# Logits blocks that contract 64 partitions each, from alternating halves, in a graph kernel on one core

## The chip, the cores and the metric

One Trainium2 chip (trn2), one core of it. The metric is the device time of one execution in microseconds (us). Before the change three executions took 1065.97, 1066.78 and 1067.74 us, median 1066.78 us.

## What is computed

Four graph layers run one after the other on 2048 nodes with 128 features, each behind a layer normalisation, a ReLU and a residual sum. The change lies in the second one, an attention with nucleus (top-p) sparsification, done twice:

```
for n in range(2):
    q = Xa @ W1.T @ W2.T                  # 2048 x 64
    k = Xa @ W3.T                         # 2048 x 64
    probs = softmax(q @ k.T)              # 2048 x 2048 logits, contracted over 64
    A = probs kept up to a mass of 0.9 per row, renormalised
    Xf = R @ Xf;  Xa = A @ Xa
    Z = Z + Xf @ U1[n].T + Xa @ U2[n].T
```

R is the row-normalised adjacency matrix plus identity. Everything is float32.

## The kernel before, in words

Each engine has its own program, written out by hand in order; semaphores tie them together. A program's order is thus the queue of its engine. The 2048 nodes are 16 tiles of 128 rows; four tiles are a group, numbered gi from 0 to 7 over the two steps of the attention.

**Keys.** The tile K (128 partitions, 2048 columns) holds the layer's input until it has been saved to memory, and then the keys. `keys_of` and, for step 1, `later_keys` (L652, L881) multiply W3 with 512 nodes and give 64 rows; ScalarE copies them (`keys_of`, L1141) to the partitions 0 to 63 of K and adds them up on the way into `ksum4`, of which `ksum` is the sum. GpSimd writes zeros to the partitions 64 to 127 of K, once (`keys_zeroed`, L453), each block after its saving DMA, and to the same partitions of ST[1] (L467). It does so between the `power` instructions that the layer normalisations wait for. TensorE waits for these zeros by `zero_ok` (L890, L899).

**Queries.** `queries` (L692) multiplies W1 with the group's 512 nodes (64 rows out), ScalarE copies them to ST[0], TensorE multiplies with W2 (L710, contracted over 64 partitions, 64 rows out), ScalarE copies the result to the partitions 0 to 63 of ST[1]. `means` (L713) multiplies the queries with `ksum` for the mean logit of each row, a column at a time; VectorE scales it by 1/2048 (L1679).

**Logits.** One tile of 128 rows has 2048 logits in each row: four matmuls of 512 columns into four neighbouring PSUM banks, L743 in `logits`, L728 in `logit_part` for the first two tiles of a step. With the zeros below, each contracts all 128 partitions. A float32 matmul stands in the trace as two weight loads (LDWEIGHTS) and two MATMUL instructions in turn, so that a tile's logits are 8 MATMULs. VectorE then takes the row maximum over the four banks (L1659, `row_max`), ScalarE the exponential (L1217). But for the first groups of a step, where tiles alternate between banks 0 to 3 and 4 to 7, all tiles use banks 0 to 3, so the logits of one tile wait until the exponential of the tile before it has left the banks.

**What runs beside them.** While the logits of group gi+1 are made, VectorE finds the thresholds of group gi by sums over 2048 elements (L1520, some of them on ScalarE, L1249) and sorted maxima (L2106), and TensorE does `attend` for the group before: for each tile it turns the kept probabilities in 4x4 transposes (L546), ScalarE copies each (L1082), and 16 matmuls follow (L808). The logits of the tiles 1 to 3 of a group stand inside `attend`, ahead of its `mults(0)` (L821); those of tile 0 stand behind the group's queries and means. In the first group of each step there is no `attend`, and units of the product R @ Xf (L612) stand between the logits.

The prologue that leads to the first logits is the first layer's product (L676), with the keys of blocks 0 and 1 and the first query (L655, L660) put between its matmuls by `MEANWHILE`. It waits for six copies of turned weights by ScalarE (`wt_ok`, L639, L1113 to L1118).

Of the kernel before, what the change touches and what calls it, by code (L numbers as in the profile page):

```python
# [14 lines left out]
P = 128  # L15
# [79 lines left out]
def gnn_kernel(nc, x, adj, W0, b0, W1, W2, W3, U1, U2, ln_g, ln_b, L2W, L3W, b3, out):  # L95
# [18 lines left out]
    with ExitStack() as ctx:  # L114
# [15 lines left out]
        XR = XT[:, :].rearrange("p (t c) -> p t c", c=P)  # L130
        keys = K[0:DA, :, :].rearrange("p t c -> p (t c)")
        wide_keys = K[:, :, :].rearrange("p t c -> p (t c)")
        ST = [sb(f"ST{i}", [P, BK]) for i in range(2)]
# [88 lines left out]
        def rows(b):  # L222
# [11 lines left out]
            sure_steps ksum_ok mean_mm mean_ok lnz_ok gap_ok guess_steps guess_ok  # L234
            cs_ok at_saved un_half un_st un_t un_row un_pr un_z th_ok sum_ok roots_ok fin_sq bias_ok h2_t h2_st hw_mm x2_ok mask_ok zero_ok
            ln_steps ln_sq ln_var ln_pow ln_root ln_y ln_t ln_ts ln_x ln_x2 h2_act diag_ok early_in x2_dma"""
# [7 lines left out]
         ksum_ok, mean_mm, mean_ok, lnz_ok, gap_ok, guess_steps, guess_ok,  # L244
         cs_ok, at_saved, un_half, un_st, un_t, un_row, un_pr, un_z, th_ok, sum_ok, roots_ok, fin_sq, bias_ok, h2_t, h2_st, hw_mm, x2_ok, mask_ok, zero_ok,
         ln_steps, ln_sq, ln_var, ln_pow, ln_root, ln_y, ln_t, ln_ts, ln_x, ln_x2, h2_act, diag_ok, early_in, x2_dma) = [sem(n) for n in names.split()]
# [185 lines left out]
        def _(pool):  # L432
# [19 lines left out]
            n += 2  # L452
            def keys_zeroed(b, count):  # L453

                pool.wait_ge(x1_dma[b], 16)
                if count > 0:
                    pool.wait_ge(zero_ok, count)
                pool.memset(K[DA:P, b * G:(b + 1) * G, :], 0.0).then_inc(zero_ok, 1)

            for b in range(NB - 1):  # L460
                power(sm[:, 3, :], sm[:, 2, :], 0, G, n + 1 + b)
            pool.wait_ge(pw_out, n + NB - 1)
            for b in range(NB - 1):
                keys_zeroed(b, b)
            pool.wait_ge(ps_t, 1 + NB)
            pool.wait_ge(zero_ok, NB - 1)
            pool.memset(ST[1][DA:P, :], 0.0).then_inc(zero_ok, 1)  # L467
            pool.wait_ge(zero_ok, NB)
            power(sm[:, 3, :], sm[:, 2, :], 0, G, n + NB)
            n += NB  # L470
            pool.wait_ge(pw_out, n)
            keys_zeroed(NB - 1, NB)
            pool.wait_ge(zero_ok, NB + 1)
            power(esc[:, :], cs[:, :], 1, NT, n + 1)
# [67 lines left out]
        def _(pe):  # L542
# [95 lines left out]

            pe.wait_ge(wt_ok, 6)  # L639

# [11 lines left out]
            def keys_of(n):  # L652

                pe.wait_ge(h_st, 1 + NB + n + 1)
                pe.matmul(bank(n)[0:DA, :], WT[:, W3T, 0:DA], XT[:, n * BK:(n + 1) * BK],  # L655
                          start=True, stop=True).then_inc(k_mm, 1)
# [5 lines left out]
            def second_query():  # L662

                pe.wait_ge(t1_out, 1)
                pe.matmul(bank(7)[0:DA, :], WT[0:DA, W2T, 0:DA], ST[0][0:DA, :], start=True, stop=True)\
                  .then_inc(q_mm, 1)
# [25 lines left out]
            def queries(step, g):  # L692
                src = XT if step == 0 else xaT
                gi = NB * step + g

                if gi - 1 in BOTH:
                    pe.wait_ge(exp_ok, G * gi)
                if gi > 0:
                    pe.wait_ge(q_out, gi)
                if gi > 2:  # L700
                    pe.wait_ge(z_ok, G * (gi - 1 if gi == NB + 1 else gi - 2))
                issued = units_by(NB * step + (1 if g == 3 else 0))
                if g == 2:
# [6 lines left out]
                pe.matmul(bank(7)[0:DA, :], WT[0:DA, W2T, 0:DA], ST[0][0:DA, :], start=True, stop=True)\  # L710
                  .then_inc(q_mm, 1)

            def means(step, g):  # L713


                gi = NB * step + g
                pe.wait_ge(q_out, gi + 1)
                pe.wait_ge(ksum_ok, step + 1)
                if gi > 0:
                    pe.wait_ge(mean_ok, gi)  # L720
                for k in range(G):
                    mm = pe.matmul(bank(6)[:, MEANS + G * (gi % 2) + k:MEANS + G * (gi % 2) + k + 1],
                                   ST[1][0:DA, k * P:(k + 1) * P], ksum[0:DA, :], start=True, stop=True)
                mm.then_inc(mean_mm, 1)

            def logit_part(k, n):

                return pe.matmul(bank(4 * k + n), ST[1][:, k * P:(k + 1) * P], wide_keys[:, n * BK:(n + 1) * BK],  # L728
                                 start=True, stop=True)

            def logits(step, g, k):
# [10 lines left out]
                for n in range(4):  # L742
                    mm = pe.matmul(bank(half(gi, k) + n), ST[1][:, k * P:(k + 1) * P],  # L743
                                   wide_keys[:, n * BK:(n + 1) * BK],
                                   start=True, stop=True)
                mm.then_inc(logits_ok, 1)
# [134 lines left out]
            def later_keys(n):  # L881

                pe.wait_ge(exT_ok, G * (n + 1))
                pe.matmul(bank(n)[0:DA, :], WT[:, W3T, 0:DA], xaT[:, n * BK:(n + 1) * BK],
                          start=True, stop=True).then_inc(k_mm, 1)

            for step in range(STEPS):
                if step == 0:
                    pe.wait_ge(q_out, 1)
                    pe.wait_ge(zero_ok, NB)  # L890
                    for n in range(3):
                        pe.wait_ge(k_out, n + 1)
                        logit_part(0, n)
                        if n < 2:
                            logit_part(1, n)
                    hr_turned(3)
                    keys_of(3)
                    pe.wait_ge(k_out, 4)
                    pe.wait_ge(zero_ok, NB + 1)  # L899
                    logit_part(0, 3).then_inc(logits_ok, 1)  # L900
                    means(0, 0)
                    logit_part(1, 3)
                    pe.wait_ge(mean_ok, 1)
                    logit_part(1, 2).then_inc(logits_ok, 1)
                    for k in range(2, G):
                        logits(0, 0, k)
                else:
                    later_keys(3)
                    pe.wait_ge(k_out, NB + 4)
                    logit_part(0, 3).then_inc(logits_ok, 1)  # L910
                    means(1, 0)
                    for n in (0, 1, 3):
                        logit_part(1, n)
                    pe.wait_ge(mean_ok, NB + 1)
                    logit_part(1, 2).then_inc(logits_ok, 1)
                    for k in range(2, G):
# [31 lines left out]
                if step == 0:  # L948
                    later_keys(2)
                    pe.wait_ge(q_out, NB + 1)  # L950
                    for n in range(3):
                        pe.wait_ge(k_out, NB + n + 1)
                        logit_part(0, n)
                    for k in range(G):
# [120 lines left out]
        def _(act):  # L1075
# [37 lines left out]
            copy(WT[:, 0, 0:DA], bank(4)[:, 0:DA]).then_inc(wt_ok, 1)  # L1113
            copy(WT[:, 1, 0:DA], bank(4)[:, P:P + DA]).then_inc(wt_ok, 1)
            copy(WT[0:DA, 2, 0:DA], bank(4)[0:DA, 2 * P:2 * P + DA]).then_inc(wt_ok, 1)
            copy(WT[:, 3, :], bank(4)[:, 3 * P:4 * P]).then_inc(wt_ok, 1)
# [24 lines left out]
            def keys_of(step, n):  # L1141

                act.wait_ge(k_mm, 4 * step + n + 1)
                act.activation(keys[:, n * BK:(n + 1) * BK], bank(n)[0:DA, :], ACT.Copy,
                               accum_out=ksum4[0:DA, n:n + 1]).then_inc(k_out, 1)

# [14 lines left out]
            act.wait_ge(q_mm, 1)  # L1161
            copy(ST[1][0:DA, :], bank(7)[0:DA, :]).then_inc(q_out, 1)
            for n in range(2, NB):
# [6 lines left out]
            def queries(step, g):  # L1170
# [4 lines left out]
                act.wait_ge(q_mm, gi + 1)  # L1175
                copy(ST[1][0:DA, :], bank(7)[0:DA, :]).then_inc(q_out, 1)

# [330 lines left out]
        def _(dve):  # L1508
# [73 lines left out]
            v(tt(XR, XR, BC[:, B0, :].unsqueeze(1).to_broadcast([P, NT, P]), ALU.add))  # L1582
            dve.wait_ge(wt_ok, 6)
            v(tt(WT[:, L2WT, :], WT[:, L2WT, :], ident[:, :], ALU.add))
# [878 lines left out]
```

## Time and profile before

| | |
|---|---|
| median of three executions | 1066.78 us (1065.97 to 1067.74) |
| span of the profiled execution, first to last instruction | 1063.4 us |
| TensorE busy, of the span | 838.8 us (79%) |
| VectorE busy | 779.5 us (73%) |
| ScalarE busy | 510.0 us (48%) |
| GpSimd busy | 69.7 us (7%) |
| mean granted clock of TensorE, of full speed | 0.899 |

The span is the only time of the profiled execution itself; the median of the timed ones is 3.4 us above it. Times in the rows below are microseconds from the span's start. In the trace's lists a row of an engine gives start, length, engine, line, operation, output and inputs with their shape, how many instructions are merged in it, and in brackets how long the engine had been idle and what released it. PEld is TensorE's weight load. A shape such as 64*128 ahead of the sizes is the part of the array that a matmul uses: contracted partitions times columns. The chain of waits is the sequence of work that ended last, followed back from the end.

### The profile page before, as it was taken

The page shows a single profiled execution, that of the slowest core. Times are in us where ns is not written, and L with a number is a line of the kernel's source. Part 1 is how long each engine was busy: PE and PEld are TensorE (multiplying, and loading weights), DVE is VectorE, ACT ScalarE, POOL GpSimd, SP SyncE. Part 2 cuts the span into 40 slices and gives each one's busy share as a digit, 9 for nine tenths or more (in the row PEclk, how much of TensorE's full clock was granted, in tenths as well). Part 3 has the DMA queues.
Part 4 walks back from the last instruction along what each step waited for, and adds up shares of the span by engine and source line. Part 5 has one row for each costly group of instructions (what it writes and reads, how often), then busy time and mean ns, then how long its engine had stood idle before and what let it go on. Part 6 is the DMA issues. An engine that isn't in the chain of part 4 may idle for free.

```text
span 1063.4 us, 12286 instructions
## 1 busy us (share of the span) xinstructions
PE 838.8 (79%) x3886; PEld 566.1 (53%) x3886; DVE 779.5 (73%) x2363; ACT 510.0 (48%) x979; POOL 69.7 (7%) x68
## 2 busy tenths in 40 slices
PE   5889958887887853939779878868658999996695
PEld 4844425655665642737256557547447475553342
DVE  5968779888987998971697899889789702326715
ACT  4877235357368376413552664674775232023212
POOL 0020110000000000000000000010001100002201
PEclk9899998998988995969799789989789999998798
DMA  9849304424004000000043320230260456500001
GB/s 339 344 174 431 119 8 151 132 106 159 1 1 159 1 0 2 1 2 1 1 158 124 108 88 1 79 136 1 59 269 15 153 238 253 221 1 0 1 0 40
DMA packets 20221, 108.25 MB, mean 102 GB/s; under 512 B 1824, under 2 KB 8752, under 8 KB 9776
## 3 DMA queue, kind: packets, MB, share of 16 engines
q1 hardware_dynamic: 18752, 106.77, 27.0%
q10 hardware_dynamic: 1392, 0.61, 0.2%
q8 instruction: 29, 0.48, 0.2%
q14 instruction: 48, 0.39, 0.1%
HBM read 88.23 MB, written 19.14 MB: 101 GB/s over the span
## 4 chain that ended last, share of the span: by engine, by line
PE 46%; DVE 27%; ACT 13%; issue 9%; POOL 2%; DMA 1%; DVEq 1%; POOLq 0%; SPq 0%; ACTq 0%
PE PS L808 10%; DVE AT L1520 8%; PE PS L743 6%; PE PS L676 5%; PE PS L546 5%; DVE mxv L1659 4%; PE PS L877 3%; ACT BC L1249 3%; ACT AT L1249 3%; DVE nd L1523 3%; PE PS L1060 3%; PE PS L1036 3%; PE PS L1066 2%; DVE AT L2106 2%; ACT AT L1082 2%
## 5 line engine op out<-in xcount | busy, mean ns | idle before, releaser
L1082 ACT ACTIVATE AT<-PS 128x512 f32<-128x512 f32 (+2 forms) x240 | 118.8, 561 | 121.3 <-PE PS L546 103.7
L743 PE MATMUL PS<-K,ST 128*128 128x512 f32 x224 | 125.6, 713 | 13.0 <-ACT EA L1217 7.6
L546 PE MATMUL PS<-ident,AT 128*128 128x128 f32 x544 | 85.5, 293 | 55.4 <-DVE rS L2161 24.5
L1520 DVE SCALAR_TENSOR_TENSOR AT<-EA,se 128x2048 uint8<-128x2048 f32 (+1 forms) x46 | 107.6, 2345 | 1.6 <-DVE se L1513 0.3
L546 PEld LDWEIGHTS PS<-ident,AT 128*128 128x128 f32 x544 | 68.7, 152 | 64.0 <-DVE rS L2161 26.1
L1520 DVE SCALAR_TENSOR_TENSOR AT<-AT 128x2048 uint8<-128x2048 f32 (+2 forms) x48 | 96.1, 2002 | 2.0 <-PE PS L546 1.1
L1659 DVE TENSOR_REDUCE mxv<-PS 128x1 f32<-128x2048 f32 x32 | 73.3, 2289 | 26.0 <-PE PS L743 20.4
L743 PEld LDWEIGHTS PS<-K,ST 128*128 128x128 f32 x224 | 49.4, 232 | 73.1 <-issue 73.0
L2106 DVE MAX8 AT<-AT 128x8 f32<-128x256 f32 x256 | 87.6, 412 | 0.7
L808 PE MATMUL PS<-hr,AT 128*128 128x128 f32 x512 | 69.8, 285 | 9.2 <-ACT AT L1082 8.4
L808 PE MATMUL PS<-AT 128*128 128x128 f32 x512 | 68.3, 281 | 8.7 <-ACT AT L1082 8.1
L808 PEld LDWEIGHTS PS<-hr,AT 128*128 128x128 f32 x512 | 64.6, 197 | 14.8 <-ACT AT L1082 12.0
L1082 ACT ACTIVATE ST<-PS 128x512 f32<-128x512 f32 (+3 forms) x43 | 23.9, 560 | 100.0 <-PE PS L1066 23.2
L808 PEld LDWEIGHTS PS<-AT 128*128 128x128 f32 x512 | 63.1, 194 | 14.8 <-ACT AT L1082 11.8
L612 PE MATMUL PS<-AT,hr 128*128 128x256 f32 x256 | 58.2, 380 | 1.6 <-ACT AT L1192 0.9
L612 PE MATMUL PS<-AT 128*128 128x256 f32 x256 | 58.0, 380 | 1.4 <-DMA AT<-keep_at 1.4
L676 PE MATMUL PS<-AT,R 128*128 128x512 f32 x128 | 56.8, 595 | 1.2 <-ACT WT L1082 1.2
L1036 PE MATMUL PS<-AT,R 128*128 128x512 f32 x128 | 57.2, 592 | 0.0
L1217 ACT ACTIVATE AT<-PS,negmax 128x2048 f32<-128x2048 f32 x16 | 31.5, 1966 | 48.8 <-DVE negmax L1517 48.8
L877 PE MATMUL PS<-AT,hr 128*128 128x512 f32 x96 | 46.0, 631 | 10.6 <-ACT hr L1355 10.6
L612 PEld LDWEIGHTS PS<-AT,hr 128*128 128x128 f32 x256 | 47.7, 190 | 11.3 <-issue 3.2
L612 PEld LDWEIGHTS PS<-AT 128*128 128x128 f32 x256 | 47.9, 190 | 10.5 <-issue 4.5
(297 smaller groups left out, 1473.1 us busy)
## 6 DMA issues: line engine op xcount, KB each, us to landing
AT<-keep_at SPq DMA_DIRECT2D x32, 1024.0 KB, 5.1
EA<-in_adj SPq DMA_DIRECT2D x20, 1024.0 KB, 6.8
keep_at<-AT SPq DMA_DIRECT2D x8, 2048.0 KB, 24.9
AT<-keep_at SPq DMA_DIRECT2D x8, 2048.0 KB, 12.3
AT<-in_adj SPq DMA_DIRECT2D x12, 1024.0 KB, 5.0
EA<-keep_degrees SPq DMA_DIRECT2D x1, 1024.0 KB, 6.5
keep_x<-K SPq DMA_DIRECT2D x4, 256.0 KB, 8.6
out<-EA SPq DMA_DIRECT2D x4, 256.0 KB, 2.3
```

Of the source, the lines that this page charges most:

```text
L546: return pe.transpose(dst, src, ident[0:p, 0:p])
L612: mm = pe.matmul(bank(6)[:, 2 * P:4 * P], left[:, j, :], slab[:, j, :], start=(j == 0), stop=(j == NT - 1))
L676: mm = pe.matmul(halves(4 + b % 2), R[:, j, :], AT[:, 2 * b:2 * b + 2, j, :], start=(j == 0), stop=(j == NT - 1))
L743: mm = pe.matmul(bank(half(gi, k) + n), ST[1][:, k * P:(k + 1) * P], wide_keys[:, n * BK:(n + 1) * BK], start=True, stop=True)
L808: mm = pe.matmul(bank(6)[:, 0:P], stg[b % 2][:, n * P:(n + 1) * P], left[:, j, :], start=(j == 0), stop=(j == NT - 1))
L877: mm = pe.matmul(bank(n), hr[:, t, :], natural(t)[:, n * BK:(n + 1) * BK], start=(t == 0), stop=(t == NT - 1))
L1036: mm = pe.matmul(halves(4 + i % 2), R[:, j, :], AT[:, 2 * b:2 * b + 2, j, :], start=(j == 0), stop=(j == NT - 1))
L1082: return act.activation(dst, src, ACT.Copy)
L1249: act.activation(act_junk[f], E[:, k, :], func, scale=-1.0, bias=th[:, k:k + 1], accum_out=below[:, f, k:k + 1]).then_inc(sum_ok, 1)
L1520: return dve.scalar_tensor_tensor(out=o, in0=x0, scalar=s, in1=x1, op0=op0, op1=op1, **k)
L1659: v(dve.tensor_reduce(mxv[:, odd:odd + 1], PS[:, b:b + 4, :], AX.XY, ALU.max))
L2106: v.put(dve.max(tops[0][:, k, s * TOP:(s + 1) * TOP], cands[k][:, s * N // SETS:(s + 1) * N // SETS]))
```

## The change

Keys and queries are made twice over: the copies of W3 and W2 stand twice in WT, so that the matmuls give 128 rows, and ScalarE copies 128 partitions. The logits matmuls of even blocks of 512 columns then contract the partitions 0 to 63, those of odd blocks 64 to 127. The means contract all 128 partitions, twice the sum, and are scaled by 0.5/2048. GpSimd's five memsets and the semaphore `zero_ok` go. ScalarE has two copies more at the weights, and `wt_ok` is waited for at 8.

```diff
-        keys = K[0:DA, :, :].rearrange("p t c -> p (t c)")
-        wide_keys = K[:, :, :].rearrange("p t c -> p (t c)")
+        keys = K[:, :, :].rearrange("p t c -> p (t c)")
...
-            for b in range(NB - 1):
+            for b in range(NB):
                 power(sm[:, 3, :], sm[:, 2, :], 0, G, n + 1 + b)
-            pool.wait_ge(pw_out, n + NB - 1)
-            for b in range(NB - 1):
-                keys_zeroed(b, b)
-            pool.wait_ge(ps_t, 1 + NB)
-            pool.wait_ge(zero_ok, NB - 1)
-            pool.memset(ST[1][DA:P, :], 0.0).then_inc(zero_ok, 1)
-            pool.wait_ge(zero_ok, NB)
-            power(sm[:, 3, :], sm[:, 2, :], 0, G, n + NB)
             n += NB
-            pool.wait_ge(pw_out, n)
-            keys_zeroed(NB - 1, NB)
-            pool.wait_ge(zero_ok, NB + 1)
...
-            pe.wait_ge(wt_ok, 6)
+            pe.wait_ge(wt_ok, 8)
...
-                pe.matmul(bank(n)[0:DA, :], WT[:, W3T, 0:DA], XT[:, n * BK:(n + 1) * BK],
+                pe.matmul(bank(n), WT[:, W3T, :], XT[:, n * BK:(n + 1) * BK],
...
-                pe.matmul(bank(7)[0:DA, :], WT[0:DA, W2T, 0:DA], ST[0][0:DA, :], start=True, stop=True)\
+                pe.matmul(bank(7), WT[0:DA, W2T, :], ST[0][0:DA, :], start=True, stop=True)\
...
-                                   ST[1][0:DA, k * P:(k + 1) * P], ksum[0:DA, :], start=True, stop=True)
+                                   ST[1][:, k * P:(k + 1) * P], ksum[:, :], start=True, stop=True)
...
-            def logit_part(k, n):
+            def logit_part(to, k, n):
 
-                return pe.matmul(bank(4 * k + n), ST[1][:, k * P:(k + 1) * P], wide_keys[:, n * BK:(n + 1) * BK],
-                                 start=True, stop=True)
+                half_rows = slice(0, DA) if n % 2 == 0 else slice(DA, P)
+                return pe.matmul(bank(to + n), ST[1][half_rows, k * P:(k + 1) * P],
+                                 keys[half_rows, n * BK:(n + 1) * BK], start=True, stop=True)
...
                 for n in range(4):
-                    mm = pe.matmul(bank(half(gi, k) + n), ST[1][:, k * P:(k + 1) * P],
-                                   wide_keys[:, n * BK:(n + 1) * BK],
-                                   start=True, stop=True)
+                    mm = logit_part(half(gi, k), k, n)
...
-                    pe.wait_ge(zero_ok, NB)
...
-                    pe.wait_ge(zero_ok, NB + 1)
...
-            copy(WT[:, 1, 0:DA], bank(4)[:, P:P + DA]).then_inc(wt_ok, 1)
-            copy(WT[0:DA, 2, 0:DA], bank(4)[0:DA, 2 * P:2 * P + DA]).then_inc(wt_ok, 1)
+            for h in range(2):
+                copy(WT[:, W3T, h * DA:(h + 1) * DA], bank(4)[:, P:P + DA]).then_inc(wt_ok, 1)
+            for h in range(2):
+                copy(WT[0:DA, W2T, h * DA:(h + 1) * DA], bank(4)[0:DA, 2 * P:2 * P + DA]).then_inc(wt_ok, 1)
...
-                act.activation(keys[:, n * BK:(n + 1) * BK], bank(n)[0:DA, :], ACT.Copy,
-                               accum_out=ksum4[0:DA, n:n + 1]).then_inc(k_out, 1)
+                act.activation(keys[:, n * BK:(n + 1) * BK], bank(n), ACT.Copy,
+                               accum_out=ksum4[:, n:n + 1]).then_inc(k_out, 1)
...
-                copy(ST[1][0:DA, :], bank(7)[0:DA, :]).then_inc(q_out, 1)
+                copy(ST[1][:, :], bank(7)).then_inc(q_out, 1)
...
-            dve.wait_ge(wt_ok, 6)
+            dve.wait_ge(wt_ok, 8)
...
-                ts(mean, PS[:, 6, MEANS + G * par:MEANS + G * par + G], 1.0 / N, ALU.mult).then_inc(mean_ok, 1)
+                ts(mean, PS[:, 6, MEANS + G * par:MEANS + G * par + G], 0.5 / N, ALU.mult).then_inc(mean_ok, 1)
...
-                total(ksum[0:DA, :], ksum4[0:DA, :]).then_inc(ksum_ok, 1)
+                total(ksum[:, :], ksum4[:, :]).then_inc(ksum_ok, 1)
```

`later_keys`, `second_query` and the calls of `logit_part` change in the same way; the order of the calls stays.

## Rows read from the trace of the kernel before

**Rows 1.** The groups of instructions by line: logits, row maxima; busy, mean ns, idle before.

```profile
L743 PE MATMUL PS<-K,ST 128*128 128x512 f32 x224 | 125.6, 713 | 13.0 <-ACT EA L1217 7.6 <-ACT AT L1217 5.4
L1659 DVE TENSOR_REDUCE mxv<-PS 128x1 f32<-128x2048 f32 x32 | 73.3, 2289 | 26.0 <-PE PS L743 20.4 <-PE PS L728 5.3
```

**Rows 2.** The chain of waits in order of time, pieces of the logits: start, length.

```profile
275.24 3.43 PE PS L743 x8
502.75 3.65 PE PS L728 x8
526.62 5.99 PE PS L743 x8
625.22 6.20 PE PS L743 x8
706.34 6.60 PE PS L743 x8
```

**Rows 3.** VectorE's list in order of time: its idle time behind those logits.

```profile
214.97 2.29 DVE L1659 TENSOR_REDUCE mxv<-PS 128x1 f32<-128x2048 f32 x1 [4.66 <-PE PS L743]
323.35 0.16 DVE L1520 SCALAR_TENSOR_TENSOR se<-below,se 128x4 f32<-128x4 f32 x1 [2.65 <-ACT BC L1249]
382.78 2.35 DVE L1520 SCALAR_TENSOR_TENSOR AT<-EA,se 128x2048 f32<-128x2048 f32 x1 [0.21 <-PE PS L546]
532.63 2.29 DVE L1659 TENSOR_REDUCE mxv<-PS 128x1 f32<-128x2048 f32 x1 [0.70 <-PE PS L743]
631.44 2.29 DVE L1659 TENSOR_REDUCE mxv<-PS 128x1 f32<-128x2048 f32 x1 [1.95 <-PE PS L743]
712.96 2.29 DVE L1659 TENSOR_REDUCE mxv<-PS 128x1 f32<-128x2048 f32 x1 [2.02 <-PE PS L743]
```

**Rows 4.** The chain of waits in the prologue: matmuls of 128 and 64 columns, first logits.

```profile
114.22 1.72 PE PS L676 x4
115.94 1.00 PE PS L655 x2
116.94 1.06 PE PS L676 x2
...
137.94 1.14 PE PS L728 x2
```

**Rows 5.** TensorE's weight loads in the same stretch, in order of time.

```profile
114.92 0.19 PEld L676 LDWEIGHTS PS<-AT,R 128*128 128x128 f32 x1 [0.24 <-issue]
116.87 0.30 PEld L676 LDWEIGHTS PS<-AT,R 128*128 128x128 f32 x2 [0.81 <-issue]
```

**Rows 6.** The groups by line: ScalarE's copies from PSUM, of 64 and of 128 partitions.

```profile
L1082 ACT ACTIVATE ST<-PS 128x512 f32<-128x512 f32 x20 | 11.9, 601 | 75.1 <-PE PS L1066 23.2 <-PE PS L1036 22.8 <-PE PS L676 14.1
L1082 ACT ACTIVATE ST<-PS 64x512 f32<-64x512 f32 x16 | 9.4, 590 | 20.8 <-PE PS L710 11.7 <-PE PS L707 6.6 <-PE PS L660 1.3
```

**Rows 7.** The chain of waits ahead of the first product: the weights' copies.

```profile
64.11 1.25 ACT WT L1082 x6
```

**Rows 8.** GpSimd's list in the prologue, in order of time.

```profile
117.33 1.80 POOL L458 MEMSET K<- 64x512 f32 x3
127.81 0.52 POOL L467 MEMSET ST<- 64x512 f32 x1 [8.68 <-PE PS L546]
132.46 1.01 POOL L445 TENSOR_TENSOR sm<-sm,ex 128x4 f32<-128x4 f32 x1 [4.13 <-DMA keep_x<-K]
133.53 0.52 POOL L458 MEMSET K<- 64x512 f32 x1
```

**Rows 9.** TensorE's list: the same run of instructions at two granted clocks.

```profile
298.32 1.31 PE L808 MATMUL PS<-hr,AT 128*128 128x128 f32 x8 [2.15 <-ACT AT L1082]
302.96 0.60 PE L546 MATMUL PS<-ident,AT 128*128 128x128 f32 x4
...
379.14 1.16 PE L808 MATMUL PS<-hr,AT 128*128 128x128 f32 x8 [2.15 <-ACT AT L1082]
382.14 0.60 PE L546 MATMUL PS<-ident,AT 128*128 128x128 f32 x4
```

More of the change, by code:

```diff
@@ L234, in gnn_kernel @@
             sure_steps ksum_ok mean_mm mean_ok lnz_ok gap_ok guess_steps guess_ok
-            cs_ok at_saved un_half un_st un_t un_row un_pr un_z th_ok sum_ok roots_ok fin_sq bias_ok h2_t h2_st hw_mm x2_ok mask_ok zero_ok
+            cs_ok at_saved un_half un_st un_t un_row un_pr un_z th_ok sum_ok roots_ok fin_sq bias_ok h2_t h2_st hw_mm x2_ok mask_ok
             ln_steps ln_sq ln_var ln_pow ln_root ln_y ln_t ln_ts ln_x ln_x2 h2_act diag_ok early_in x2_dma"""
@@ L244, in gnn_kernel @@
          ksum_ok, mean_mm, mean_ok, lnz_ok, gap_ok, guess_steps, guess_ok,
-         cs_ok, at_saved, un_half, un_st, un_t, un_row, un_pr, un_z, th_ok, sum_ok, roots_ok, fin_sq, bias_ok, h2_t, h2_st, hw_mm, x2_ok, mask_ok, zero_ok,
+         cs_ok, at_saved, un_half, un_st, un_t, un_row, un_pr, un_z, th_ok, sum_ok, roots_ok, fin_sq, bias_ok, h2_t, h2_st, hw_mm, x2_ok, mask_ok,
          ln_steps, ln_sq, ln_var, ln_pow, ln_root, ln_y, ln_t, ln_ts, ln_x, ln_x2, h2_act, diag_ok, early_in, x2_dma) = [sem(n) for n in names.split()]
@@ L452, in _ @@
             n += 2
[L453 to L458, printed above, removed]
-            for b in range(NB - 1):
-                power(sm[:, 3, :], sm[:, 2, :], 0, G, n + 1 + b)
-            pool.wait_ge(pw_out, n + NB - 1)
-            for b in range(NB - 1):
-                keys_zeroed(b, b)
-            pool.wait_ge(ps_t, 1 + NB)
-            pool.wait_ge(zero_ok, NB - 1)
-            pool.memset(ST[1][DA:P, :], 0.0).then_inc(zero_ok, 1)
-            pool.wait_ge(zero_ok, NB)
-            power(sm[:, 3, :], sm[:, 2, :], 0, G, n + NB)
+            for b in range(NB):
+                power(sm[:, 3, :], sm[:, 2, :], 0, G, n + 1 + b)
             n += NB
-            pool.wait_ge(pw_out, n)
-            keys_zeroed(NB - 1, NB)
-            pool.wait_ge(zero_ok, NB + 1)
             power(esc[:, :], cs[:, :], 1, NT, n + 1)
@@ L709, in queries @@
                 pe.wait_ge(t1_out, gi + 1)
-                pe.matmul(bank(7)[0:DA, :], WT[0:DA, W2T, 0:DA], ST[0][0:DA, :], start=True, stop=True)\
+                pe.matmul(bank(7), WT[0:DA, W2T, :], ST[0][0:DA, :], start=True, stop=True)\
                   .then_inc(q_mm, 1)
@@ L883, in later_keys @@
                 pe.wait_ge(exT_ok, G * (n + 1))
-                pe.matmul(bank(n)[0:DA, :], WT[:, W3T, 0:DA], xaT[:, n * BK:(n + 1) * BK],
+                pe.matmul(bank(n), WT[:, W3T, :], xaT[:, n * BK:(n + 1) * BK],
                           start=True, stop=True).then_inc(k_mm, 1)
@@ L889, in _ @@
                     pe.wait_ge(q_out, 1)
-                    pe.wait_ge(zero_ok, NB)
                     for n in range(3):
                         pe.wait_ge(k_out, n + 1)
-                        logit_part(0, n)
+                        logit_part(0, 0, n)
                         if n < 2:
-                            logit_part(1, n)
+                            logit_part(4, 1, n)
                     hr_turned(3)
@@ L898, in _ @@
                     pe.wait_ge(k_out, 4)
-                    pe.wait_ge(zero_ok, NB + 1)
-                    logit_part(0, 3).then_inc(logits_ok, 1)
+                    logit_part(0, 0, 3).then_inc(logits_ok, 1)
                     means(0, 0)
-                    logit_part(1, 3)
+                    logit_part(4, 1, 3)
                     pe.wait_ge(mean_ok, 1)
-                    logit_part(1, 2).then_inc(logits_ok, 1)
+                    logit_part(4, 1, 2).then_inc(logits_ok, 1)
                     for k in range(2, G):
@@ L909, in _ @@
                     pe.wait_ge(k_out, NB + 4)
-                    logit_part(0, 3).then_inc(logits_ok, 1)
+                    logit_part(0, 0, 3).then_inc(logits_ok, 1)
                     means(1, 0)
                     for n in (0, 1, 3):
-                        logit_part(1, n)
+                        logit_part(4, 1, n)
                     pe.wait_ge(mean_ok, NB + 1)
-                    logit_part(1, 2).then_inc(logits_ok, 1)
+                    logit_part(4, 1, 2).then_inc(logits_ok, 1)
                     for k in range(2, G):
@@ L952, in _ @@
                         pe.wait_ge(k_out, NB + n + 1)
-                        logit_part(0, n)
+                        logit_part(0, 0, n)
                     for k in range(G):
@@ L1175, in queries @@
                 act.wait_ge(q_mm, gi + 1)
-                copy(ST[1][0:DA, :], bank(7)[0:DA, :]).then_inc(q_out, 1)
+                copy(ST[1][:, :], bank(7)).then_inc(q_out, 1)
             def unit_sums(u):
```

## The prediction

> **What bounds the kernel now.** I read the groups by line first, to see how much of TensorE's work is logits and who waits for it; then the chain of waits, to see which of these logits set the end; then VectorE's own list, to see how far each could shrink before something else is last; and the prologue in all lists, for what the other edits touch.
>
> The groups show 32 row maxima, one for each tile of logits, and VectorE idle for 20.4 + 5.3 = 25.7 us in all because they waited for the tile's matmuls [rows 1]. Apart from single matmuls in the prologue the chain holds 17 whole tiles of logits, of 3.4 to 6.6 us each; five of them stand in the rows, the other twelve repeat these patterns [rows 2]. A tile that follows other work closely takes 3.43 us, which is 0.43 us for each of its 8 MATMULs, so TensorE runs at its upper level, 2.4 GHz, there; those with 5.99 to 6.60 us ran mostly at half of it. VectorE is the other half of the story: between the logits it is busy without a pause, so a tile can give back only what VectorE idles behind it [rows 3]. Attention is thus bound by VectorE and TensorE in turn, and a faster logits tile pays at ten places, listed below, not 32 times.
>
> **The change part by part.** *The overlap.* Nothing before the change shows two matmuls on different halves, so this cost must be bounded. At worst the two halves run one after the other: 8 x 0.43 us, as now. At best every MATMUL shares its time with one of the other half: 4 x 0.43 = 1.72 us. I take a value between, from the order of the instructions. Call the two MATMULs of an even block A1, A2 and of an odd block B1, B2. They are issued A1 A2 B1 B2 A1 A2 B1 B2. I assume that they start in order, that two of one half follow each other, and that two of different halves may run together. Then the tile is A1, A2 with B1, B2 with A1, A2 with B1, B2: five steps of 0.43, 2.15 us.
>
> *The switch.* Where a matmul of another shape comes between, a pair of MATMULs takes 1.00 us instead of 0.86 on the way in, and 1.06 on the way back [rows 4]; the next weights are then not loaded ahead but in twos, after a pause of 0.81 us instead of 0.24 [rows 5]. This was another shape, 64 columns and not 64 partitions; I take its 0.14 and 0.20 us as the nearest. The tile behind the 64-partition means shows the same size: 3.65 against 3.43 us [rows 2]. Between free and twice that the price is 0 to 0.68 us; I take 0.34, since logits stand amid 128-partition work. A tile then takes 2.15 + 0.34 = 2.49 us, **0.95 us** less than 3.44. At half clock it is 5 x 0.86 + 0.34 = 4.6 us.
>
> *The places.* Five times two tiles follow each other through TensorE, with units or an attend between: 198 and 211, 275 and 286 us, and the same pattern at 559 and 573, 639 and 650, 720 and 732. VectorE idles 4.66 us behind the first pair and 2.65 behind the second, by way of ScalarE's sums [rows 2, 3], so 2 x 0.95 = 1.9 fits each time: 9.5 us. The pair at 356 and 367 gives 0.2, because VectorE had waited only 0.21 us for what follows and is last from there [rows 3]. At the start of step 1 the tile at 502.75 has its blocks in the order even, odd, odd, even, six steps: 2.58 + 0.34 against 3.65, 0.7 us; the tile after the next, 3.69 us long in the chain, gives 0.95; VectorE idled some 2 us for each; together 1.7. The tile at 526.62 gives the 0.70 that VectorE idled, whatever it saves. The two at half clock, 625 and 706, save 6.20 - 4.6 = 1.6 and 6.60 - 4.6 = 2.0, against 1.95 and 2.02 us of idle time. Sum: 9.5 + 0.2 + 1.7 + 0.7 + 1.6 + 2.0 = **15.7 us**. The other logits of L743 end while VectorE is busy, and give nothing.
>
> *Keys and queries with 128 columns.* The matmuls are as long as before. In the prologue the two key matmuls lose the switches in and out: 2 x (0.14 + 0.20) = 0.7 us off the chain [rows 4]. ScalarE copies 128 partitions in 601 ns and 64 in 590 [rows 6]; sixteen copies of the queries and keys on the path would be 0.2 us, which I leave out. The means contract 128 partitions: still one column at a time, nothing.
>
> *Two copies more at the weights.* Six take 1.25 us on the chain, so two more cost 2 x 0.2 = 0.4 us [rows 7]. VectorE waits for the same count, and its next work lies behind the same product.
>
> *No zeros.* The memsets are 1.80 + 0.52 + 0.52 us. The three end 8.68 us before the next; that one is over at 128.33, four microseconds before `power` starts; the last comes behind `power` and is over at 134.05, while the logits that need it only start at 137.94 [rows 4, 8]. All stand in waits of GpSimd for others; no DMA moves, and the keys still wait for the saving DMAs. Worth nothing.
>
> *The clock.* TensorE will idle more. The same instructions, each behind 2.15 us of idle time, took 4.64 us from the first row to the last in one group and 3.00 in the next [rows 9]: one fall to half clock there costs 1.6 us. Longer pauses arise where logits end earlier but VectorE is not faster, near 262 and 343 us. I count about one such fall on the path, 1 us net; with a fall at each of the ten places it would be 16, with none nothing.
>
> The sum is 15.7 + 0.7 - 0.4 - 1 = 15 us. It is made on a span of 1063.4 us; the timed runs lie 3.4 us above at 1066.8, so the forecast is 1066.8 - 15 = **1052 us**.
>
> **The rivals.** *Full pairing.* If both MATMULs of a block pair off, a tile is 4 x 0.43 + 0.34 = 2.06 us and saves 1.38: five pairs 13.8, the rest capped as above 0.2 + 2.4 + 0.7 + 1.95 + 2.02, and 0.3 from the prologue, 21 us, **1045 us**. For it: the matmuls are independent and write different banks. Against it: the two MATMULs of one block need different weights in the same rows and are issued one behind the other. The Trainium skill, "TensorE: Matmul & The Clock Gate", section on packing small matmuls, says that matmuls on separate row groups start within some 4 ns of each other; by that rule taken plainly the time would be this rival's. No row before the change shows it.
>
> *No overlap, the other side.* The place is the border between the even and the odd block in `logit_part`: if the odd block's first MATMUL waits until the even block's second has ended, every tile keeps its 8 x 0.43 us and pays the switch of 0.34. On the path that is five pairs 3.4, the pair at 356 0.7, and five single tiles 1.7, less 0.3: +5.5 us, **1072 us**. It decides as soon as a tile has more than seven steps (7 x 0.43 + 0.34 = 3.35 against 3.44 us). For it: the trace shows TensorE starting matmuls strictly one behind the other, and stopping its weight loads ahead whenever the shape changes [rows 5]. Against it: only that the halves share no rows. Were each change of half a switch of its own, four times 0.17 us more per tile would make it some 1082.
>
> The skill's page "TensorEngine Tiling (Array Packing)", key properties, says that a change of tiling mode drains the array while a change of tile does not; by that rule the 1082 is not to be expected. The trace agrees for the first half, with the 0.14 and 0.20 us above.
>
> *The gain is eaten.* The overlap works, but TensorE's longer pauses drop its clock at most of the ten places, 16 us lost against 16 gained [rows 9]: **1067 us**, no change.
>
> **How the numbers follow.** My forecast (five steps) has a chance of 0.42, full pairing 0.15, the eaten gain 0.13, no overlap 0.25 and its far end 0.05. What a measurement can tell from no change is about 0.2%, 2.1 us. Faster is 0.42 + 0.15 = 0.57, the same 0.13, slower 0.30. The forecast's own range is 1046 to 1058, from a free switch to a switch twice as dear. The range to hold the time 8 times in 10 reaches from 1043, full pairing with a cheaper switch, to 1073, no overlap.
>
> **What would show it.** In the changed profile a tile of logits inside attend (now 3.43 us) should take about 2.5 us, with MATMULs of shape 64*128 from two halves running at once; 2.1 would be full pairing, 3.8 no overlap. VectorE's 25.7 us of waiting for logits should fall to some 15, and its wait for ScalarE's sums near 323 us from 2.65 to below 1. GpSimd's prologue should end no earlier at the following products. The mean granted clock (0.899) should stay above 0.87. The prediction is wrong if a tile stays at 3.4 us or more, or if tiles shrink and VectorE's idle time only moves elsewhere.

## The result and the profile after

The changed kernel took 1051.59 us (median of four executions, 1046.53 to 1055.7), the kernel before 1066.71 us beside it: a ratio of 0.9853, 95% interval 0.9822 to 0.9884, **15 us less**. Timed again later, in five executions, it took 1048.47 us (1047.12 to 1051.94) against 1067.35, ratio 0.9832 (0.9812 to 0.9852). The profiled execution took 1052.0 us with a span of 1050.2, 13.2 us below the span of before. The mean granted clock fell from 0.899 to 0.877, and the executions of the changed kernel lie 9 us apart where those of before lay within 2.

The groups by line first, as in [rows 1]; after the bar stand busy time, mean ns, and the idle time ahead with its releasers:

```profile
L710 PE MATMUL PS<-K,ST 64*128 64x512 f32 x256 | 91.5, 810 | 17.4 <-ACT EA L1197 10.9 <-ACT AT L1197 4.1 <-ACT K L1124 1.6
L1639 DVE TENSOR_REDUCE mxv<-PS 128x1 f32<-128x2048 f32 x32 | 73.2, 2288 | 15.1 <-PE PS L710 14.7
```

The logits (now all on L710) have the shape 64*128, and VectorE waits 14.7 us for them where it waited 25.7 [rows 1]. TensorE's list shows a tile of logits between other work:

```profile
270.79 1.16 PE L788 MATMUL PS<-hr,AT 128*128 128x128 f32 x8 [1.15 <-ACT AT L1060]
271.78 1.15 PE L527 MATMUL PS<-ident,AT 128*128 128x128 f32 x9
272.86 1.99 PE L710 MATMUL PS<-K,ST 64*128 64x512 f32 x8
274.77 1.16 PE L788 MATMUL PS<-hr,AT 128*128 128x128 f32 x8
```

From the tile's first MATMUL to the mults (L788) behind it 1.91 us pass. The single records give the starts: 272.857 and 272.864, 273.391 and 273.397, 273.820 and 273.826, 274.249 and 274.256. Four pairs, 6 or 7 ns apart inside a pair and 0.43 us from the second pair to the third and to the fourth: **full pairing**, four steps and not five. The Trainium skill, "TensorE: Matmul & The Clock Gate", Part 3 on packing small matmuls, puts the starts of matmuls on separate row groups some 4 ns apart; the trace agrees but for 2 to 3 ns. Where a block has no neighbour on the other half it runs alone: the tile at the start of step 1 [rows 2, 502.75] has its blocks in the order even, odd, odd, even, and the last waits for VectorE's means. Its first two blocks pair, the other two follow one by one, six steps in all: it went from 3.65 to 2.79 us in the chain.

```profile
498.97 2.79 PE PS L710 x8
```

The keys in the prologue lost their switches as predicted: what took 1.00 and 1.06 us [rows 4] takes 0.86 each.

```profile
115.59 0.86 PE PS L636 x2
116.45 0.86 PE PS L657 x2
```

**Where the gain lies.** The table compares the distance between row maxima (the same two in both kernels) around each place of the prediction; positive is time gained. "Again" is the profile of the changed kernel's second timing, span 1046.7 us.

| place (times of before) | predicted | after | again |
|---|---|---|---|
| start of the program to the fifth row maximum | 0.3 and the clock | 0.26 | -1.86 |
| pair 198 and 211 | 1.9 | 2.22 | 1.89 |
| pair 275 and 286 | 1.9 | 2.43 | **-0.19** |
| pair 356 and 367, to the start of step 1 | 0.2 | -0.96 | -0.29 |
| start of step 1 | 1.7 | 2.53 | 2.53 |
| 526 | 0.7 | 0.70 | 0.71 |
| pair 559 and 573 | 1.9 | 2.32 | 2.94 |
| 625 | 1.6 | 1.93 | 2.42 |
| pair 639 and 650 | 1.9 | **-1.78** | 0.80 |
| 706 | 2.0 | 2.06 | 2.12 |
| pair 720 and 732, and all behind it | 1.9 | 1.64 | 5.63 |

The rows add up to the 13.2 and 16.7 us of the spans but for 0.2 us between them.

Each profile has one pair that loses time where it gains time in the other profile. In the first it is 639 and 650. The row maximum ahead of it starts 5.1 us before the mults that begin each of these two lists; before, then after:

```profile
636.55 1.16 PE L808 MATMUL PS<-AT 128*128 128x128 f32 x8 [1.60 <-ACT AT L1082]
637.55 1.04 PE L546 MATMUL PS<-ident,AT 128*128 128x128 f32 x8
638.42 0.27 PE L546 MATMUL PS<-ident,T 128*128 128x128 f32 x1
638.53 3.60 PE L743 MATMUL PS<-K,ST 128*128 128x512 f32 x8
641.97 1.05 PE L808 MATMUL PS<-AT 128*128 128x128 f32 x8
```

```profile
625.29 2.07 PE L788 MATMUL PS<-AT 128*128 128x128 f32 x8 [3.52 <-ACT AT L1060]
627.16 1.91 PE L527 MATMUL PS<-ident,AT 128*128 128x128 f32 x8
628.86 0.42 PE L527 MATMUL PS<-ident,T 128*128 128x128 f32 x1
629.22 3.02 PE L710 MATMUL PS<-K,ST 64*128 64x512 f32 x8
632.17 1.16 PE L788 MATMUL PS<-AT 128*128 128x128 f32 x8
```

The logits ahead had ended sooner, the copies that release L788 had not, so TensorE paused 3.52 us where it had paused 1.60. Behind it the transposes and most of the logits run at half clock. The windows of these two stretches (length, busy time of PE, PEld, DVE, ACT and POOL, then the granted clock) say the same; before, then after:

```profile
636.50:642.00 5.50, 5.45 (x26) 3.53 (x27) 5.33 (x13) 1.62 (x5) 0.00 (x0) 1.00 0.01 3
```

```profile
625.30:632.20 6.90, 6.90 (x26) 4.79 (x26) 6.52 (x23) 1.73 (x4) 0.00 (x0) 0.56 0.01 2
```

From mults to mults it is 5.42 us before and 6.88 after, although the tile itself holds half as many steps. In the second profile this place has a pause of only 1.17 us and stays at 2.4 GHz; there it is the pair at 275 that stands behind a pause of 3.69 us:

```profile
273.07 2.08 PE L788 MATMUL PS<-hr,AT 128*128 128x128 f32 x8 [3.69 <-ACT AT L1060]
274.94 2.13 PE L527 MATMUL PS<-ident,AT 128*128 128x128 f32 x9
277.00 3.09 PE L710 MATMUL PS<-K,ST 64*128 64x512 f32 x8
...
628.41 1.16 PE L788 MATMUL PS<-AT 128*128 128x128 f32 x8 [1.17 <-ACT AT L1060]
```

Over the whole stretch of the logits the clock fell too; before, then after:

```profile
130.00:830.00 700.00, 530.21 (x2654) 384.87 (x2653) 589.65 (x1737) 375.88 (x656) 25.56 (x27) 0.88 0.20 68
```

```profile
130.00:830.00 700.00, 514.80 (x2702) 381.37 (x2698) 595.41 (x1757) 380.67 (x676) 29.02 (x29) 0.84 0.20 71
```

With two levels, 0.88 means that 24% of these 700 us were at 1.2 GHz, 168 us, and 0.84 means 224. My theory after this reading: the pairing is worth some 21 us, and longer pauses at half clock give 2 to 6 of them back. The rivals: the other edits bring the gain; matmuls start in order after all; VectorE and not the clock caps it.

### The profile page after: what moved, and what is told of

It is laid out like the page before. It is cut to its first block, busy times and chain, and to the rows that moved or that the text cites. A ratio compares the mean times of both kernels' runs of the same rounds, so it can differ in the third digit from the quotient of the medians.

```text
span 1050.2 us, 12275 instructions
## 1 busy us (share of the span) xinstructions
PE 811.1 (77%) x3886; PEld 556.4 (53%) x3886; DVE 778.6 (74%) x2363; ACT 510.8 (49%) x981; POOL 68.0 (6%) x63
## 4 chain that ended last, share of the span: by engine, by line
PE 38%; DVE 37%; ACT 11%; issue 9%; POOL 2%; DVEq 1%; DMA 1%; POOLq 0%; SPq 0%; ACTq 0%
DVE AT L1500 13%; PE PS L788 8%; PE PS L657 5%; DVE mxv L1639 5%; PE PS L527 4%; PE PS L857 3%; DVE AT L2086 3%; DVE nd L1503 3%; ACT BC L1229 3%; PE PS L1038 3%; PE PS L1014 3%; PE PS L710 3%; ACT AT L1229 2%; PE PS L1044 2%; DVE se L1493 2%
## 5 line engine op out<-in xcount | busy, mean ns | idle before, releaser
L710 PE MATMUL PS<-K,ST 64*128 64x512 f32 x256 | 91.5, 810 | 17.4 <-ACT EA L1197 10.9
L1639 DVE TENSOR_REDUCE mxv<-PS 128x1 f32<-128x2048 f32 x32 | 73.2, 2288 | 15.1 <-PE PS L710 14.7
L788 PE MATMUL PS<-AT 128*128 128x128 f32 x512 | 72.4, 292 | 12.5 <-ACT AT L1060 12.0
L788 PE MATMUL PS<-hr,AT 128*128 128x128 f32 x512 | 72.8, 293 | 8.5 <-ACT AT L1060 7.5
L788 PEld LDWEIGHTS PS<-AT 128*128 128x128 f32 x512 | 65.9, 202 | 21.4 <-ACT AT L1060 17.1
L788 PEld LDWEIGHTS PS<-hr,AT 128*128 128x128 f32 x512 | 66.2, 203 | 17.7 <-ACT AT L1060 11.7
L593 PE MATMUL PS<-AT,hr 128*128 128x256 f32 x256 | 61.4, 395 | 5.1 <-DVE gs L1497 4.2
L593 PE MATMUL PS<-AT 128*128 128x256 f32 x256 | 61.3, 394 | 2.8 <-DVE gs L1497 1.6
L710 PEld LDWEIGHTS PS<-K,ST 64*128 64x128 f32 x256 | 30.7, 240 | 52.3 <-issue 45.1
L593 PEld LDWEIGHTS PS<-AT 128*128 128x128 f32 x256 | 49.0, 197 | 16.7 <-issue 6.0
```

The lines of the kernel that those rows point to most:

```text
L593: mm = pe.matmul(bank(6)[:, 2 * P:4 * P], left[:, j, :], slab[:, j, :], start=(j == 0), stop=(j == NT - 1))
L710: return pe.matmul(bank(to + n), ST[1][half_rows, k * P:(k + 1) * P], keys[half_rows, n * BK:(n + 1) * BK], start=True, stop=True)
L788: mm = pe.matmul(bank(6)[:, 0:P], stg[b % 2][:, n * P:(n + 1) * P], left[:, j, :], start=(j == 0), stop=(j == NT - 1))
L1639: v(dve.tensor_reduce(mxv[:, odd:odd + 1], PS[:, b:b + 4, :], AX.XY, ALU.max))
```

## The experiments

### What brings the gain: one half only, and all rows

`one_half` takes the second half away and leaves all else:

```diff
-                half_rows = slice(0, DA) if n % 2 == 0 else slice(DA, P)
+                half_rows = slice(0, DA)
```

> Every block of logits contracts the partitions 0 to 63, so that no two matmuls can run side by side; the doubled keys and queries, the missing zeros and the copies stay as in the changed kernel. If the overlap of the two halves is what the change is worth, a tile inside attend takes 8 x 0.43 us and the two switches, some 3.8 us instead of 2.1, and the time is that of the kernel before or some us above it, 1066 to 1073 us. If the other edits bring the gain, it stays near 1052.

`all_rows` contracts all 128 partitions of the doubled keys and queries:

```diff
-                half_rows = slice(0, DA) if n % 2 == 0 else slice(DA, P)
+                half_rows = slice(0, P)
...
-                copy(WT[0:DA, W2T, h * DA:(h + 1) * DA], bank(4)[0:DA, 2 * P:2 * P + DA]).then_inc(wt_ok, 1)
+                act.activation(WT[0:DA, W2T, h * DA:(h + 1) * DA], bank(4)[0:DA, 2 * P:2 * P + DA], ACT.Copy,
+                               scale=0.5).then_inc(wt_ok, 1)
...
-                ts(mean, PS[:, 6, MEANS + G * par:MEANS + G * par + G], 0.5 / N, ALU.mult).then_inc(mean_ok, 1)
+                ts(mean, PS[:, 6, MEANS + G * par:MEANS + G * par + G], 1.0 / N, ALU.mult).then_inc(mean_ok, 1)
```

> The logits contract all 128 partitions of the doubled keys and queries; the second weights stand in at half their value, so that the doubled sum is the same logit (and the means are scaled by 1/2048). No zeros, no overlap, and no change of the matmuls' shape between the logits and the rest. If the overlap brings the gain, the time is that of the kernel before less the 1 us of the prologue: 1064 to 1067 us, with logits of 3.44 us a tile. If the missing zeros and the shapes of the keys bring it, it is near 1052.

`all_rows` took 1068.12 us, ratio 1.0012 (1.0001 to 1.0022), with tiles of 3.44 us and 26.4 us of VectorE's waiting, as before. Missing zeros, doubled keys and two copies more are thus worth nothing, about 1 us on the wrong side: the rival of the other edits falls, and **the overlap brings the whole gain**.

`one_half` took 1116.4 us, ratio 1.0476 (1.0445 to 1.0506), which neither theory had said. Its tiles at 2.4 GHz are what was expected, 3.63 us to the next work where before has 3.43. But 16 of its 32 tiles took 7.0 us or more. TensorE's list, with a tile behind a pause and one behind busy work:

```profile
202.61 0.69 PE L527 MATMUL PS<-ident,AT 128*128 128x128 f32 x2 [3.04 <-ACT AT L1060]
203.09 1.06 PE L616 MATMUL PS<-WT,AT 128*128 128x128 f32 x4
204.09 7.19 PE L710 MATMUL PS<-K,ST 64*128 64x512 f32 x8
211.21 1.22 PE L593 MATMUL PS<-AT,hr 128*128 128x256 f32 x2
...
607.80 3.70 PE L710 MATMUL PS<-K,ST 64*128 64x512 f32 x8
```

The windows give the clock of that tile and of the next:

```profile
204.09:211.20 7.11, 7.11 (x9) 2.50 (x8) 3.18 (x6) 0.62 (x2) 0.00 (x0) 0.50 0.00 1
222.30:225.90 3.60, 3.60 (x9) 1.42 (x8) 0.00 (x0) 0.80 (x4) 0.00 (x0) 1.00 0.71 262
```

A tile of before that begins at half clock gets the full clock on its way ([rows 2]: 5.99 to 6.60 us, not 6.9). Here it stays at 0.50 to its end.

### What a tile on one half does to the clock

`one_half_filled` adds to `one_half` the unused matmuls of `fill_all` below.

> All blocks from the partitions 0 to 63, as in one_half, with the unused matmuls of fill_all in the pauses. If a tile of one_half takes 7.2 us because the clock is already down when it begins and does not rise within it, the tiles behind the fills take 3.7 us, and the time is well below one_half's 1116: the six or so tiles that the fills reach save 3.5 us each, 1090 to 1100 us. If a tile on one half brings the clock down by itself, the tiles stay at 7.2 us and the time stays above 1110.

1100.27 us, ratio 1.0297 (1.0272 to 1.0323), 16 us less. The tile of 7.19 us above now stands behind added matmuls instead of a pause:

```profile
200.43 4.63 PE L731 MATMUL PS<-ident 128*128 128x128 f32 x40
204.89 0.38 PE L527 MATMUL PS<-ident,AT 128*128 128x128 f32 x2
205.11 0.61 PE L616 MATMUL PS<-WT,AT 128*128 128x128 f32 x4
205.65 3.70 PE L710 MATMUL PS<-K,ST 64*128 64x512 f32 x8
```

3.70 us: behind busy work at 2.4 GHz such a tile keeps the full clock, but where the clock is down it does not raise it. Whether it can bring the clock down is not settled: three tiles of these two runs begin at 1.00 and end at 0.50 (4.94, 5.16 and 6.74 us), and they stand behind pauses of 0.5 to 1.7 us. The tiles that the added matmuls do not reach stay at 7.0 to 7.2 us, 12 of them. So the half clock accounts for the size of `one_half`'s loss: 16 tiles at 3.5 us more than 3.63 are 56 us, and it lost 49.

### In order, or a line for each half

`evens_first` changes the order of the blocks in `logits`, and nothing else:

```diff
-                for n in range(4):
+                for n in (0, 2, 1, 3):
```

> Only the order of a tile's four blocks inside the logits of the tiles from the second group on changes: both even blocks first, then both odd ones. If each half of the partitions has its own line of matmuls, the first odd one starts beside the first even one or a step behind it at most, and a tile stays near 2.0 us at 2.4 GHz. If matmuls start strictly in the order in which they are issued, the odd ones start only when the fourth even one starts, and a tile takes 6 or 7 steps of 0.43 us, 2.8 to 3.2 us; at some six tiles of the chain that is 5 to 7 us over the changed kernel.

One execution, 1051.72 us. A tile behind busy work, with its neighbours:

```profile
274.20 1.15 PE L527 MATMUL PS<-ident,AT 128*128 128x128 f32 x9
275.28 1.99 PE L710 MATMUL PS<-K,ST 64*128 64x512 f32 x8
277.20 1.16 PE L788 MATMUL PS<-hr,AT 128*128 128x128 f32 x8
```

1.99 us, to the hundredth that of the changed kernel, though four MATMULs of one half are issued ahead of the first of the other. The single records again start in four pairs, 13 to 14 ns apart inside a pair. The start in order is refuted: each half has a line of its own.

### Does the clock give back part of the gain?

`fill_first` keeps TensorE busy in the pause ahead of the last mults of a group's first tile, with matmuls whose results nobody reads:

```diff
+            def filled(count, to, col=0):
+
+                for _ in range(count):
+                    pe.matmul(bank(to)[:, col:col + P], ident[:, :], ident[:, :], start=True, stop=True)
...
                 mults(2)
+                filled(fill[1], 4)
                 mults(3)
...
+                                   fill=(0, (4, 10)[step] if more and k == 0 else 0))
```

> TensorE gets matmuls whose results nobody uses (ident times ident into bank 4, four in step 0 and ten in step 1), in attend for the first tile of a group, where it otherwise waits for ScalarE's copy ahead of the last mults. The pauses there of 3.3 to 3.6 us near 625 and 706 us shrink below 2.5. If the clock's falls behind the longer pauses give back part of the gain, the matmuls behind these two pauses run at 2.4 GHz (1.0 us for eight transposes instead of 1.9) and the time is 2 to 6 us below the changed kernel's. If VectorE sets the pace there whatever TensorE's clock is, the time is the same within 1 us. If the added matmuls are in the way, it is 1 to 2 us above.

1050.43 us (1048.45 to 1051.54), ratio 0.9845 (0.9820 to 0.9870): not to be told from the changed kernel, so the 2 to 6 us did not come. The place itself does what was expected:

```profile
625.06 2.40 PE L731 MATMUL PS<-ident 128*128 128x128 f32 x20
627.29 1.06 PE L793 MATMUL PS<-AT 128*128 128x128 f32 x8
628.19 1.04 PE L527 MATMUL PS<-ident,AT 128*128 128x128 f32 x8
629.06 0.27 PE L527 MATMUL PS<-ident,T 128*128 128x128 f32 x1
629.26 1.99 PE L710 MATMUL PS<-K,ST 64*128 64x512 f32 x8
```

No pause, no half clock, and the pair at 639 gains 0.78 us instead of losing 1.78. But the second profile of the changed kernel gains 0.80 there without help.

`fill_all` adds two more places:

```diff
+                if early and u == units_by(NB * step) + 1:
+                    pe.wait_ge(un_z, u)
+                    filled(20, 7, 2 * P)
...
+                filled(fill[0], 6)
                 mults(0)
...
+                                   fill=(6 if more and k == G - 1 else 0, (4, 10)[step] if more and k == 0 else 0))
```

> As the one before, with such matmuls also ahead of the mults of a group's last tile (six into bank 6) and behind the second early unit of each step (twenty of them into bank 7), where the pauses are 2.2 us and more. If the clock gives back part of the gain, the share of the time at half clock between 130 and 830 us falls from about 220 us to below 150, and the time is 5 to 10 us below the changed kernel's, some 1043 us. If VectorE caps the gain, the time is that of the changed kernel within 1 us, at a higher granted clock.

1045.96 us, ratio 0.9792 (0.9762 to 0.9821). The clock in the window of 700 us rose to 0.86 only, that is some 196 us at half clock and not below 150; the time fell by as much as I had said. To see that it was not chance, it ran again (`fill_again`) beside the changed kernel (`after_again`), together with the control that the theory needs: the same matmuls in the kernel before (`before_filled`, the same diff).

> The changed kernel as it is, timed beside the next three. Its runs so far lay between 1046.5 and 1055.7 us, those of the kernel before within 1.8 us. If the clock's falls behind TensorE's pauses differ from execution to execution, it spreads over several us again, around 1051.

> The kernel of fill_all once more, beside the changed kernel. If the unused matmuls keep the clock from falling, it is 4 to 7 us below the changed kernel; if the first result was the spread of the runs, the two are the same within 2 us.

> The kernel before, with the same unused matmuls at the same three places. If the clock's loss was brought by the change, through pauses that became longer, the fills give little here: the three tiles of the chain at half clock (526, 625, 706 us) can give at most 0.70 + 1.95 + 2.02 = 4.7 us by VectorE's idle time behind them, and the two at 198 and 559 us some 1 us each; I expect 2 to 4 us less than the kernel before, 1063 to 1065. If the clock cost the kernel before as much as the changed one, it is 5 to 7 us less, 1060 to 1062. Both say that it stays above 1055, far from the changed kernel.

| | us, median of five | ratio to before, 95% |
|---|---|---|
| kernel before | 1067.35 (nine) | |
| before_filled | 1058.07 | 0.9914 (0.9898 to 0.9929) |
| after_again | 1048.47 | 0.9832 (0.9812 to 0.9852) |
| fill_again | **1044.25** | 0.9786 (0.9768 to 0.9805) |

The added matmuls give the changed kernel 4.2 us and the kernel before 9.3. That is a miss for both of my sums, the theory's 2 to 4 and the other's 5 to 7: the half clock that these matmuls can win back had cost the kernel before more, not less. The overlap is worth 18.9 us without them and 13.8 with them. The two gains cover each other where VectorE's waiting is all there is to win. At 625 and 706 VectorE had idled 1.95 and 2.02 us [rows 3]; the faster clock alone (the profile of before_filled) gains 2.43 and 2.06 us there, the overlap alone 1.93 and 2.06, and both together (fill_again) 2.41 and 2.05.

`fill_half` asks whether it matters what TensorE is busy with:

```diff
-                    pe.matmul(bank(to)[:, col:col + P], ident[:, :], ident[:, :], start=True, stop=True)
+                    pe.matmul(bank(to)[:, col:col + P], ident[0:DA, :], ident[0:DA, :], start=True, stop=True)
```

> As fill_all, but the unused matmuls contract the partitions 0 to 63 alone: as many, as long, as busy. If it is enough that TensorE is busy through the pause, the matmuls behind them run at 2.4 GHz as in fill_all, near 1046 us. If a matmul on one half does not hold the clock as one on all 128 partitions does, as the half-clock tiles of one_half (7.2 us where 3.7 was expected) suggest, the eight transposes behind the fills take 1.9 us again instead of 1.04, and the time is near the changed kernel's 1051 us or above it, since the added matmuls then take twice their time too.

```profile
621.38 2.50 PE L731 MATMUL PS<-ident 64*128 64x128 f32 x20
623.81 1.16 PE L796 MATMUL PS<-AT 128*128 128x128 f32 x8
624.80 1.04 PE L527 MATMUL PS<-ident,AT 128*128 128x128 f32 x8
```

The transposes behind run at 2.4 GHz. 1047.26 us, ratio 0.9818 (0.9802 to 0.9833), 3 us above fill_again: in a pause, matmuls on one half hold the clock as well. At 198 and 211, 559 and 573, 625 and 706 its profile gains what that of fill_again gains, within 0.1 us; the rest is 0.7 us less at 275 and 286, 0.95 less between 371 and 502 and 1.0 less behind the last row maximum.

### Is it VectorE?

At the pair 639 and 650 even the undisturbed profiles gain no more than 0.80 us, with tiles of 1.99. VectorE's list shows why. Its one wait of over half a microsecond for others between the row maxima at 631 and 688, before, and the same one in the second profile of the changed kernel:

```profile
685.26 0.16 DVE L1520 SCALAR_TENSOR_TENSOR se<-below,se 128x4 f32<-128x4 f32 x1 [2.74 <-ACT BC L1249]
```

```profile
676.31 0.16 DVE L1500 SCALAR_TENSOR_TENSOR se<-below,se 128x4 f32<-128x4 f32 x1 [2.02 <-ACT BC L1229]
```

Of 2.74 us only 0.72 were TensorE's; the 2.02 that are left stand behind ScalarE's own sums. So the rival of the cap is right at this place. In the first profile the half clock adds two new waits there, one of them for transposes:

```profile
653.86 0.16 DVE L1493 TENSOR_TENSOR se<-gs 128x4 f32<-128x4 f32 x1 [0.51 <-ACT gs L1214]
655.87 2.35 DVE L1500 SCALAR_TENSOR_TENSOR AT<-AT 128x2048 f32<-128x2048 f32 x1 [1.34 <-PE PS L527]
```

With the wait for ScalarE's sums, 2.79 us in that profile, they make 4.64 us of waiting against 2.74 before: 1.90 lost; the table has 1.78.

## Why the prediction was right, and where it was not

The number, 1052 against 1051.59, is right by errors that cancel: too little for a tile, too much for one pair and, in the first timing, too little for the clock. That is partly luck.

**The step that failed first** is "I assume that they start in order, that two of one half follow each other": five steps and a tile of 2.49 us. The halves run independently: four steps. From the transposes ahead of a tile to the end of the mults behind it before took 637.55 to 642.86, 5.31 us, and the second profile of after 629.40 to 633.39, 3.99: a tile saves 1.32 and not 0.95 us. That is four steps, 1.72, less 0.40 for the switches, so the switch term of 0.34 was nearly right. That is the rival of full pairing, to which I gave 0.15 because no row showed it; the tile is its tile, the time is not.

**The clock** was the second: "one such fall on the path, 1 us net". Full pairing sums to 21 us; the two timings gave 15.1 and 18.9. Some 2 of the 21 were not to be had, because 639 and 650 can give 0.80 and not 2 x 1.38 (above); of the rest 4 us are missing in the first timing and next to nothing in the second. One fall costs 2.6 us where it lands (the difference between the two profiles at 275, 2.43 against -0.19, and at 639, 0.80 against -1.78). The profile of after had the fall at 639 and a second one at 706.52 behind a pause of 3.27 us (granted clock 0.57 from 706 to 710 us), where the second profile has a pause of 1.39 and 1.00; and it lost 0.96 us between 371 and 502 us, where the granted clock was 0.79 against 0.83. It isn't true, though, that the change lost more to the clock than the kernel before had: added matmuls gave that one 9.3 us and the changed one 4.2.

**"The same pattern at 559 and 573, 639 and 650, 720 and 732"** failed with the reading behind it, 2.65 us of waiting for ScalarE's sums at 323 us [rows 3]. After the change 1.95 us of that wait are left (318.60) and at the other pair 2.02 of 2.74, since nearly all of it is ScalarE's own: it gives 0.7 us at either pair, and the expectation that it falls below 1 us failed. The pair at 275 and 286 gained 2.43 all the same, because VectorE, which the prediction has "busy without a pause" between the logits, had waited twice more there, behind the half clock of [rows 9, 298.32]:

```profile
301.83 0.17 DVE L1513 TENSOR_TENSOR se<-gs 128x4 f32<-128x4 f32 x1 [0.67 <-ACT gs L1234]
303.60 2.35 DVE L1520 SCALAR_TENSOR_TENSOR AT<-AT 128x2048 f32<-128x2048 f32 x1 [1.10 <-PE PS L546]
```

In the profile of after the same stretch falls to half clock too and takes 4.63 us from 293.26, but it begins 5.42 us behind the row maximum ahead of it and not 8.16, earlier by about two tiles of 1.32. Both waits are gone. `before_filled`, without the overlap, wins 1.64 us there by the clock. At 639 and 650 the kernel before has no such waits, and only the 0.7 is left.

The gain of 720 and 732 appears behind the last row maximum, before and after:

```profile
750.97 0.16 DVE L1513 TENSOR_TENSOR AT<-gs 128x4 f32<-128x4 f32 x1 [4.44 <-ACT gs L1234]
```

```profile
736.78 0.16 DVE L1493 TENSOR_TENSOR AT<-gs 128x4 f32<-128x4 f32 x1 [2.20 <-ACT gs L1214]
```

In the second profile 0.60 us are left. Of the 3.84 that went there, 1.44 are a fall to half clock that the kernel before has and neither profile of the changed one (L864 to L772 take 3.45 us from 746.01 in the chain of before, and 2.01 in that of after), and the other 2.4 are about two tiles; the first profile lost 1.6 of them to the fall at 706.52. The rest of the table's last row, 1.0 us lost in one profile and 1.4 gained in the other, lies behind 832 us, where no logits run.

Right by their own steps: 526, 625 and 706, which VectorE's idle time caps, each within 0.4 us in the profile of after; VectorE's wait for logits (15 expected, 14.7); the mean granted clock (above 0.87 expected, 0.877); the zeros at nothing (`all_rows`); the keys' switches. 198 and 211 gave 2.22 for 1.9, with tiles that saved more than was counted. The start of step 1 gave 2.53 and not 1.7: three tiles with 0.84 or 0.85 us each, not two. The two weight copies, counted at 0.4 us, were not on the path: the product now starts behind VectorE's R, at 65.06 where it was 65.41. No overlap, and the eaten gain as a whole, are refuted.

What stays open: why the same kernel's pauses fall differently from one execution to the next. Whether the pause is 1.17 or 3.52 us goes with when the tile ahead of it ended, and no run here fixes that moment.

## What to carry to other kernels

Two matmuls that contract 64 partitions each cost little more than one here, from different halves and into different banks, in both orders that were tried; the price is about 0.2 us at each border to matmuls of another shape. (Two halves into one bank were not tried.) Read what each place can give from the waits of the engine behind it, one by one: a pattern that repeats in the program did not repeat in the waits. And an engine that ends sooner pauses longer: look at the granted clock behind the pause, and try unused matmuls in it (here 4.2 us for the changed kernel, and 9.3 for the one before).

## What was not expected of the hardware

- The two halves keep lines of their own: 1.99 us a tile with the blocks in the order even, even, odd, odd as with even, odd, even, odd.
- A tile on one half alone that begins at 1.2 GHz stays there for its 7.2 us, where those on 128 partitions in the kernel before end at 2.4 GHz; short matmuls on one half in a pause nevertheless held 2.4 GHz (1.04 us for eight transposes behind them). What tells the two apart was not tried.
- Executions of the changed kernel spread from 1046.5 to 1055.7 us, those of before from 1065.2 to 1069.4, and the same pair of tiles gains 2.43 us in one profile and loses 0.19 in another.
